# Graph layer 0: small VectorE steps on slot counts moved within the per-graph step

## The chip, the cores and the metric

One core of one Trainium2 chip runs the whole kernel. The metric is device time in microseconds (us) for one execution. TensorE (PE) does the matmuls, VectorE (DVE) the elementwise work, ScalarE (ACT) activations and copies, GpSimd (POOL) some additions, and SyncE (SP) starts the loads.

## What is computed

Four graph layers run on 128 graphs (B) of 128 nodes (N) with 64 features (F). Only layer 0 is touched. With H = 192 it is

```python
mask = (adj > 0.0).astype(x.dtype)
xj_proj = x @ W1a                                   # W1a, W1b: [64, 192]
diff = x[:, :, None, :] - x[:, None, :, :]
h = relu(xj_proj[:, :, None, :] + diff @ W1b + b1)  # one row per pair of nodes
hm = einsum('bjkh,bjk->bjh', h, mask)               # sum over the neighbours
x  = x + hm @ W2 + deg[..., None] * b2
```

where x on the right is the layer-normalised, rectified input. Since `diff @ W1b` splits into a term of the node and one of the neighbour, the kernel computes one 128x384 product a graph and then, for each node, adds up rectified sums over its neighbours.

## The kernel before, in words

**Neighbours as slots.** A node's neighbours are numbered. A chunk is eight slots (SC = 2 SU, SU = 4): a one-hot matrix per slot, made by VectorE (`dve_onehot`, L707, 128x1024), picks neighbour rows by matmul (L441, for a high and a low half-precision part) into PSUM. Four slots are a half, which fills two of the four `slot_banks`. VectorE then does `acc += min(psum, 0)` on a half: the half sum, L725. The second chunk does not start from zero: VectorE takes the difference of its one-hot from the last one (`dve_difference`, L719), so PE adds only the change. Neighbours that do not fit in a node's own chunks go to shared slots (L434 with `host`, the one-hot L713).

**The step of a graph.** Graphs come in groups of four (GS = 4), q = 0 to 3. The trace has four half sums for each of the 128 graphs, so the chunk loop (`Fori`) runs once a graph; this text calls its two half sums the loop's first and second, and the other two the last first and the last second. PE in one step: seeds from `ident` (L434), first half (eight matmuls L441), product for graph b+2 (L401), second half, `halfway`, in the loop the two halves of the difference, `between` with the transposes of the last graph's sum (L415 to L420), the shared seeds and gathers. VectorE: one-hot, one-hot of the next chunk, `gap`, difference, loop's first and second half sum, `halfway`, last first half sum, `middle`, shared one-hot, `beside`, last second half sum, `summed`, `late`, and the next graph's one-hot.

**Order and waits.** Each engine's order is as written; engines meet at semaphores. `s_free[k]` says that half k was summed, so PE can write that pair of banks again: PE's seeds of a step wait for the last second half sum of the step before, and each half of the difference waits for the half sum before it on the same banks. `s_done[k]` says that PE filled half k.

**Counting and host rows.** Beside the four steps of a group, one part a step, the kernel works out for the next group how many chunks and shared slots its nodes need: q = 0 degrees; `dve_rows` rows per candidate; PE `pe_sum_rows` (L365); `dve_full`, `dve_count_full`, `dve_own`, `dve_left`, `dve_pieces`, `dve_pads`; PE `pe_first_rows` (L371); `dve_first_rows` (start, end, shift); `dve_from_first` (L690) and `dve_host_rows` (L699), which make the 128x512 matrix `host`. PE needs `host` in `pe_host_ranks` (L386 to L393) in the fourth step. The last group has no next one, so this runs beside 31 groups. The loop over groups holds two (u = 0, 1) in each pass.

Of the kernel before, what the change touches and what calls it, by code (L numbers as in the profile page):

```python
# [12 lines left out]
def gnn_stack_kernel(nc, a, out):  # L13
# [35 lines left out]
    with ctx:  # L49
# [88 lines left out]
        degp = sb("degp", [N, GS])  # L138
        over = sb("over", [N, GS, NC])
        rounded = sb("rounded", [N, GS, NC])  # L140
# [4 lines left out]
        least = sb("least", [N, GS])  # L145
# [4 lines left out]
        end = sb("end", [N, GS])  # L150
# [141 lines left out]
        s_from = sem("rows_from_first_made")  # L292
# [322 lines left out]
        def dve_rows(dve, g):  # L615

            v = nc.vector
            dve.wait_ge(s_dc, g + 1)
            v.scalar_tensor_tensor(out=over[:, :, :], in0=pSmall[:, 0:GS].unsqueeze(2).broadcast_to([N, GS, NC]),
                                   scalar=1.0 / SS, in1=cand[:, :].unsqueeze(1).broadcast_to([N, GS, NC]),  # L620
                                   op0=ALU.mult, op1=ALU.subtract).then_inc(s_nop, 1)
            v.tensor_scalar(degp[:, :], pSmall[:, 0:GS], float(SS - 1), None, ALU.add).then_inc(s_degp, 1)
            dve.wait_ge(s_nop, 9 * g + 1)
            v.tensor_scalar(rounded[:, :, :], over[:, :, :], 1.0 / SS, WHOLE, ALU.max, ALU.add).then_inc(s_nop, 1)
            dve.wait_ge(s_nop, 9 * g + 2)
            v.tensor_scalar(rows_or[:, :, :], rounded[:, :, :], WHOLE, None, ALU.subtract).then_inc(s_rows, 1)

        def dve_full(dve, g):

            v = nc.vector  # L630
            dve.wait_ge(s_sum, g + 1)
            v.tensor_scalar(over[:, :, :], pSmall.rearrange("p (q c) -> p q c", q=GS), float(N), None, ALU.is_gt)\
             .then_inc(s_nop, 1)

        def dve_count_full(dve, g):

            v = nc.vector
            dve.wait_ge(s_nop, 9 * g + 3)
            v.tensor_reduce(nfull[:, :], over[:, :, :], AX.X, ALU.add).then_inc(s_nop, 1)

        def dve_own(dve, g):

            v = nc.vector
            dve.wait_ge(s_nop, 9 * g + 4)
            v.tensor_scalar(chunks[:, ds(g * GS, GS)], nfull[0:1, :], 1.0, None, ALU.add)

            v.tensor_scalar(own[:, :], nfull[:, :], float(SC), float(SC * MINC), ALU.mult, ALU.add).then_inc(s_nop, 1)

        def dve_left(dve, g):

            v = nc.vector
            dve.wait_ge(s_degp, g + 1)
            dve.wait_ge(s_nop, 9 * g + 5)
            v.tensor_tensor(left[:, :], degp[:, :], own[:, :], ALU.subtract).then_inc(s_nop, 1)

        def dve_pieces(dve, g):

            v = nc.vector
            dve.wait_ge(s_nop, 9 * g + 6)
            v.tensor_scalar(least[:, :], left[:, :], float(SS - 1), -1.0, ALU.max, ALU.add).then_inc(s_nop, 1)  # L660
            dve.wait_ge(s_nop, 9 * g + 7)
            v.tensor_scalar(whole[:, :], least[:, :], 1.0 / SS, WHOLE, ALU.mult, ALU.add).then_inc(s_nop, 1)
            dve.wait_ge(s_nop, 9 * g + 8)
            v.tensor_scalar(pieces[:, :], whole[:, :], WHOLE, None, ALU.subtract).then_inc(s_pieces, 1)

        def dve_pads(dve, g, p):

            v = nc.vector
            dve.wait_ge(s_pieces, g + 1)
            v.scalar_tensor_tensor(out=pad[:, :], in0=pieces[:, :], scalar=-float(SS), in1=left[:, :],  # L670
# [129 lines left out]
        with nc.Block() as block:  # L800
# [15 lines left out]
            def _(pe):  # L816
# [23 lines left out]
                def step(b, g, u, q, nxt, p, use):  # L840
# [4 lines left out]
                    def halfway():  # L845
                        if nxt is not None:
# [6 lines left out]
                            if q == 2:  # L853
                                pe_first_rows(pe, nxt)
# [863 lines left out]
```

## Time and profile before

| | us |
|---|---|
| median of 3 runs | 1464.27 |
| lowest to highest | 1462.46 to 1469.56 |
| profiled execution | 1462.28 |
| its span | 1460.6 |
| PE busy | 1320.8 (90%) |
| DVE busy | 1176.9 (81%) |
| ACT busy | 1108.5 (76%) |
| POOL busy | 498.5 (34%) |

Layer 0 fills roughly the first 1000 us. Times in a timeline count from the span's start. A row gives start, duration, engine, line, operation, what is written and read, and how many were merged; starts are the better measure of a rate, since an instruction's recorded duration reaches a little into the next. `[0.20 <-PE ...]` is idle time ahead and what ended it.

### The profile page before, as it was taken

To read this page: it belongs to the slowest core of one execution; us is meant where nothing else is said; L and a number is where in the kernel's file an instruction comes from. 1 tells how busy PE (TensorE), PEld (TensorE's weight loads), DVE (VectorE), ACT (ScalarE), POOL (GpSimd) and SP (SyncE) were. 2 spreads that over 40 slices of the span, in tenths; PEclk is the share of its full clock that TensorE was granted. 3 is DMA by queue.
4 is the path that set the end of the run, shared out by engine and by line. 5 is a ranking of instruction groups with operands and counts; after the bars stand their busy time and mean duration, and the time that the engine had idled before them with its cause. 6 is when DMAs were issued, how large, how long until landed. Compare 5 with 4: busy or idle time off the path is not lost. (4 is left out here: it accounts for less than half of the span.)

```text
span 1460.6 us, 41314 instructions
## 1 busy us (share of the span) xinstructions
PE 1320.8 (90%) x11243; PEld 1073.9 (74%) x11244; DVE 1176.9 (81%) x3034; ACT 1108.5 (76%) x2426; POOL 498.5 (34%) x611
## 2 busy tenths in 40 slices
PE   3999999999999999999999999997999997972398
PEld 1777778777787777777778777775889887910398
DVE  7899998999999998999989999984444445978755
ACT  4788888888888888888888888873555555916676
POOL 1343344443334444434344443332222111066400
PEclk9999999999999999999999999998999998986599
DMA  7000000000000000000000000000000000000022
GB/s 153 23 10 9 7 8 14 7 7 7 7 14 7 7 7 8 13 7 7 7 14 7 7 7 7 0 2 1 1 0 0 0 0 0 0 1 0 4 54 57
DMA packets 40925, 18.11 MB, mean 12 GB/s; under 512 B 19572, under 2 KB 40886, under 8 KB 40886
## 3 DMA queue, kind: packets, MB, share of 16 engines
q1 hardware_dynamic: 40354, 17.42, 4.9%
q8 instruction: 19, 0.31, 0.1%
q10 hardware_dynamic: 532, 0.21, 0.1%
q14 instruction: 20, 0.16, 0.0%
HBM read 13.44 MB, written 4.19 MB: 12 GB/s over the span
## 5 line engine op out<-in xcount | busy, mean ns | idle before, releaser
L725 DVE SCALAR_TENSOR_TENSOR acc<-slot_banks,acc 128x768 f32<-128x768 f32 x512 | 487.2, 952 | 58.2 <-PE slot_banks L441 50.8
L794 POOL TENSOR_TENSOR acc<-acc 128x384 f32<-128x384 f32 x128 | 128.2, 1001 | 551.1 <-DVE onediff L719 543.6
L441 PE MATMUL slot_banks<-ac_hi,work 128*128 128x192 f16 x1408 | 264.9, 247 | 12.1 <-DVE work L707 10.2
L441 PE MATMUL slot_banks<-ac_lo,work 128*128 128x192 f16 x1408 | 263.8, 246 | 0.0
L441 PEld LDWEIGHTS slot_banks<-ac_hi,work 128*128 (+1 forms) x1408 | 137.1, 97 | 79.1 <-issue 58.6
L441 PE MATMUL slot_banks<-ac_hi,onediff 128*128 128x192 f16 x1024 | 183.1, 246 | 2.7
L441 PE MATMUL slot_banks<-ac_lo,onediff 128*128 128x192 f16 x1024 | 182.2, 246 | 0.0
L441 PEld LDWEIGHTS slot_banks<-ac_lo,work 128*128 (+1 forms) x1408 | 138.0, 98 | 22.7 <-issue 16.9
L541 ACT ACTIVATE work<-bank 128x512 f16<-128x512 f32 x256 | 130.7, 601 | 1.2 <-PE bank L352 1.2
L780 POOL TENSOR_TENSOR ac_lo<-ac,ac_hi 128x384 f16<-128x384 f32 x128 | 118.8, 929 | 32.4 <-ACT ac_hi L581 32.4
L707 DVE TENSOR_SCALAR work<-work,slot_key 128x1024 f16 x256 | 117.6, 479 | 9.5 <-issue 1.0
L598 ACT ACTIVATE work<-slot_banks 128x576 f32<-128x576 f32 x128 | 83.4, 651 | 49.2 <-PE slot_banks L441 47.9
L589 ACT ACTIVATE acc<-ac,neg_pad 128x768 f32<-128x768 f32 x128 | 119.3, 932 | 0.0
L441 PEld LDWEIGHTS slot_banks<-ac_hi,onediff 128*128 x1024 | 104.8, 102 | 13.0 <-issue 11.3
L580 ACT ACTIVATE ac<-bank 128x384 f32<-128x384 f32 x128 | 62.2, 486 | 66.4 <-PE bank L401 66.4
L605 ACT ACTIVATE slot_banks<-ac 128x768 f32<-128x768 f32 x127 | 103.5, 815 | 11.6
L401 PE MATMUL bank<-wac,hT 65*128 65x384 f32 x256 | 109.5, 510 | 1.7 <-ACT ac_hi L581 1.1
L441 PEld LDWEIGHTS slot_banks<-ac_lo,onediff 128*128 x1024 | 100.2, 98 | 0.0
L1220 POOL TENSOR_TENSOR adjT_all<-adjT_all,ident 128x512 f32 x32 | 39.9, 1268 | 173.4 <-PE slot_banks L1174 173.4
L1141 ACT ACTIVATE onediff<-x_all,nmr,rstd 128x64 f32 (+1 forms) x256 | 90.7, 429 | 7.4 <-PE slot_banks L1312 3.2
L719 DVE TENSOR_TENSOR onediff<-work x128 | 88.5, 692 | 7.5 <-DVE work L707 0.6
L434 PE MATMUL slot_banks<-ac_hi,ident 128*128 128x384 f16 x258 | 85.1, 330 | 9.9 <-issue 8.5
(260 smaller groups left out, 3303.3 us busy)
## 6 DMA issues: line engine op xcount, KB each, us to landing
adj_in<-in_adj_dram SPq DMA_DIRECT2D x32, 256.0 KB, 2.8
out_dram<-acc SPq DMA_DIRECT2D x32, 128.0 KB, 2.0
l1w<-in_L_gnn_W_dram SPq DMA_DIRECT2D x2, 64.0 KB
l1b<-in_L_gnn_b_dram SPq DMA_DIRECT2D x2, 64.0 KB
x_all<-in_x_dram SPq DMA_DIRECT2D x4, 0.2 KB, 11.7
nm_in<-in_nodemask_dram ACTq DMA_DIRECT2D x1, 64.0 KB
w1a<-in_L_gnn_W_dram ACTq DMA_DIRECT2D x1, 48.0 KB
w1b<-in_L_gnn_W_dram ACTq DMA_DIRECT2D x1, 48.0 KB
```

The lines of the kernel that those rows point to most:

```text
L401: nc.tensor.matmul(pAC[:, 0:2 * H], hT0[:, p, q * N:(q + 1) * N], wac[:, :], start=True, stop=True)\
L434: nc.tensor.matmul(unit(pair, t, n), node, part[:, q, 0:H].unsqueeze(1).broadcast_to([N, n, H]), start=(e == 0), stop=False)
L441: last = nc.tensor.matmul(unit(pair, t, 1), hot(t), part[:, q, H:2 * H].unsqueeze(1), start=False, stop=(e == 1 and (t % SB == SB - 1 or t ...
L541: last = nc.scalar.activation(rs[:, p, :, t, :], pA3[:, :].rearrange("p (q j) -> p q j", q=GS), ACT.Copy, bias=-float(t))
L589: nc.scalar.activation(acc[:, q, :].rearrange("p (t h) -> p t h", t=SU), ac32[:, q, 0:H].unsqueeze(1).broadcast_to([N, SU, H]), ACT.Relu, ...
L605: nc.scalar.activation(unit((q + 1) % 2, 0, SU), ac32[:, q, 0:H].unsqueeze(1).broadcast_to([N, SU, H]), ACT.Copy).then_inc(s_seed, 1)
L707: nc.vector.tensor_scalar(onehot[:, ds(at, CH)], ranks.rearrange("p t j -> p (t j)"), slot_key[:, ds(key, 1)], None, ALU.is_equal).then_in ...
L719: nc.vector.tensor_tensor(onediff[:, ds(at, CH)], onehot[:, ds(at, CH)], onehot[:, ds(at_old, CH)], ALU.subtract).then_inc(s_D, 1)
L725: nc.vector.scalar_tensor_tensor(out=sums, in0=unit((q + k) % 2, 0, SU), scalar=0.0, in1=sums, op0=ALU.min, op1=ALU.add).then_inc(s_free[k ...
L780: nc.gpsimd.tensor_tensor(ac_lo[:, q, :], ac32[:, q, :], ac_hi[:, q, :], ALU.subtract)\
L794: nc.gpsimd.tensor_tensor(acc[:, q, 0:2 * H], acc[:, q, 0:2 * H], acc[:, q, 2 * H:4 * H], ALU.add)
L1141: ins = nc.scalar.activation(hn[:, u, SLOT[q] * F:(SLOT[q] + 1) * F], x[:, ds((b + q) * F, F)], ACT.Relu, bias=nmr[:, ds(b + q, 1)], scale ...
```

## The change

What `dve_rows`, `dve_full` and so on did is cut into single instructions, each put in another place. VectorE's callback `gap` (between the second one-hot and the difference) and a new one, `hole` (between the loop's two half sums), take a link each; `late` now comes behind the next graph's one-hot. The four-instruction `dve_host_rows` becomes two 128x512 ones, a comparison (`dve_inside`) and a product. One link fewer is needed for `pieces`. On PE, `pe_sum_rows` and `pe_first_rows` go from `halfway` to `between`, and `pe_h` goes behind `pe_update`.

```diff
-        def dve_pieces(dve, g):
...
-            v.tensor_scalar(least[:, :], left[:, :], float(SS - 1), -1.0, ALU.max, ALU.add).then_inc(s_nop, 1)
...
+        def dve_excess(dve, g):
...
+            return nc.vector.scalar_tensor_tensor(out=excess[:, :], in0=nfull[:, :], scalar=-float(SC) / SS,
+                                                  in1=share[:, :], op0=ALU.mult, op1=ALU.add)
+        def dve_whole():
+            return nc.vector.tensor_scalar(whole[:, :], excess[:, :], 0.0, WHOLE, ALU.max, ALU.add)
...
-        def dve_host_rows(dve, g, p):
-            dve.wait_ge(s_from, g + 1)
-            for q in range(GS):
-                rows = host[:, p, q * N:(q + 1) * N]
-                last = nc.vector.scalar_tensor_tensor(out=rows, in0=row16[:, :], scalar=end[:, q:q + 1], in1=rows,
-                                                      op0=ALU.is_lt, op1=ALU.mult)
-            last.then_inc(s_host, 1)
+        def dve_inside(dve, g):
+            dve.wait_ge(s_first, g + 1)
+            return nc.vector.tensor_tensor(inside.rearrange("p (q j) -> p q j", q=GS),
+                                           row16[:, :].unsqueeze(1).broadcast_to([N, GS, N]),
+                                           end[:, :].unsqueeze(2).broadcast_to([N, GS, N]), ALU.is_lt)
+        def dve_host_rows(p):
+            nc.vector.tensor_tensor(host[:, p, :], host[:, p, :], inside, ALU.mult).then_inc(s_host, 1)
...
                 dve_onehot(dve, rs[:, u, q, :, :], c + 1, pos)
+                gap()
...
-                gap()
                 dve.wait_ge(s_G, cnt)
                 dve_difference(dve, pos, old)
                 dve.wait_ge(s_done[0], prev)
                 dve_half(0, q)
+                dve.wait_ge(s_free[0], prev)
+                hole()
                 dve.wait_ge(s_done[1], prev)
-                dve.wait_ge(s_free[0], prev)
                 dve_half(1, q)
...
             dve_half(1, q)
             summed()
-            late()
             if not (known(b) and b == B - 1):
                 dve.wait_ge(s_rs, g1 + 1)
                 dve_onehot(dve, rs[:, p1, q1, :, :], 0, pos)
+            late()
...
                             if q == 1:
                                 pe.wait_ge(s_h, nxt + 1)
-                                pe_sum_rows(pe, nxt)
-                                pe_h(pe, nxt)
+                                pe.wait_ge(s_degp, nxt + 1)
...
+                        if nxt is not None and q == 1:
+                            pe_h(pe, nxt)
                     def between():
                         if not (known(b) and b < 1):
                             pe_transpose_sum(pe, b - 1, *group_of(b, g, u, q, 1))
...
+                            if q == 1:
+                                pe_sum_rows(pe, nxt)
+                            if q == 2:
+                                pe_first_rows(pe, nxt)
```

Where VectorE's links stand now: `halfway` rows (q = 1), pieces (2), host rows (3); `middle` own (2); `beside` full (1), left and first rows (2); `summed` count full (1), pads (2); behind the next one-hot degrees (0), negative pads (2); `gap` over (1), excess (2), from first (3); `hole` share and rounded (1), whole (2), inside (3).

VectorE in the third step of a group (q = 2), from the loop's end to the last half sum. `pieces`, `left`, `own` and `pad` are counts for the next group, `start`, `end` and `shift` come from PE's `first rows` matmul, L713 (L726 in the changed file) is the shared one-hot and L725 (L738) a half sum. Before:

```order
L771 TENSOR_TENSOR x_all<-bank,x_all 128x64
L670 SCALAR_TENSOR_TENSOR pad<-pieces,left 128x4
L725 SCALAR_TENSOR_TENSOR acc<-slot_banks,acc 128x768
L677 TENSOR_SCALAR neg_pad<-pad 128x4
L682 COPY start<-bank 128x4
L683 TENSOR_TENSOR end<-bank,pieces 128x4
L684 SCALAR_TENSOR_TENSOR shift<-bank,own 128x4
L713 TENSOR_SCALAR work<-work,slot_key 128x384
L725 SCALAR_TENSOR_TENSOR acc<-slot_banks,acc 128x768
```

and now:

```order
L785 TENSOR_TENSOR x_all<-bank,x_all 128x64
L660 TENSOR_SCALAR pieces<-whole 128x4
L738 SCALAR_TENSOR_TENSOR acc<-slot_banks,acc 128x768
L665 TENSOR_SCALAR chunks<-nfull 1x4
L666 TENSOR_SCALAR own<-nfull 128x4
L726 TENSOR_SCALAR work<-work,slot_key 128x384
L672 SCALAR_TENSOR_TENSOR left<-deg,own 128x4
L692 COPY start<-bank 128x4
L693 TENSOR_TENSOR end<-bank,pieces 128x4
L694 SCALAR_TENSOR_TENSOR shift<-bank,own 128x4
L738 SCALAR_TENSOR_TENSOR acc<-slot_banks,acc 128x768
```

The three instructions that read the matmul's result went from ahead of the shared one-hot to behind it, still ahead of the last half sum.

PE at the same place: the matmul L371 and its neighbours, the update (L426, L427) and the transposes (L415 to L420). Before:

```order
L441 MATMUL slot_banks<-ac_lo,work 128x192
L371 MATMUL bank<-pieces,before 128x4
L426 MATMUL bank<-w2a,hmTa 128x64
L427 MATMUL bank<-w2b,hmTb 128x64
```

and now:

```order
L418 MATMUL bank<-ident,acc 128x128 x2
L420 MATMUL bank<-work,hm 128x128
L371 MATMUL bank<-pieces,before 128x4
L434 MATMUL slot_banks<-ac_hi,host 128x2x192
```

The matmul moved behind the difference's sixteen matmuls and the four transposes.

VectorE in the loop of the fourth step (q = 3) before, where L278 is a layer-norm statistic and L719 the difference:

```order
L278 BN_STATS bn<-x_all 128x6
L718 ISA
L719 TENSOR_TENSOR onediff<-work 128x1024
L725 SCALAR_TENSOR_TENSOR acc<-slot_banks,acc 128x768 x2
L734 REGISTER_ALU
L734 COMPARE_AND_BRANCH
L750 TENSOR_LOAD chunks
L771 TENSOR_TENSOR x_all<-bank,x_all 128x64
L699 SCALAR_TENSOR_TENSOR host<-row,end,host 128x128 x4
```

and now:

```order
L701 TENSOR_SCALAR host<-row,start 128x128 x4
L279 BN_STATS bn<-x_all 128x6
L751 ISA
L731 ISA
L732 TENSOR_TENSOR onediff<-work 128x1024
L738 SCALAR_TENSOR_TENSOR acc<-slot_banks,acc 128x768
L708 TENSOR_TENSOR work<-row,end 128x512
L738 SCALAR_TENSOR_TENSOR acc<-slot_banks,acc 128x768
```

`from first` (L701) came in ahead of the difference and `inside` (L708) between the half sums; the four L699 behind the loop are one product now.

## Rows read from the trace of the kernel before

**Rows 1.** Timeline of PE: first seed matmul of steps (two groups).

```profile
489.07 0.33 PE L434 MATMUL slot_banks<-ac_hi,ident 128*128 128x384 f16 x1
...
519.34 0.33 PE L434 MATMUL slot_banks<-ac_hi,ident 128*128 128x384 f16 x1 [0.55 <-issue]
...
533.53 0.33 PE L434 MATMUL slot_banks<-ac_hi,ident 128*128 128x384 f16 x1
...
540.94 0.33 PE L434 MATMUL slot_banks<-ac_hi,ident 128*128 128x384 f16 x1
...
549.14 0.33 PE L434 MATMUL slot_banks<-ac_hi,ident 128*128 128x384 f16 x1
```

**Rows 2.** Timeline of PE, end of step q = 1: shared seeds start behind the transposes.

```profile
532.36 0.33 PE L434 MATMUL slot_banks<-ac_hi,host 128*128 128x384 f16 x1
```

**Rows 3.** Timeline of DVE: last half sum of q = 1, the two one-hots behind it.

```profile
532.39 0.95 DVE L725 SCALAR_TENSOR_TENSOR acc<-slot_banks,acc 128x768 f32<-128x768 f32 x1
...
534.07 1.08 DVE L707 TENSOR_SCALAR work<-work,slot_key 128x1024 f16 x2
```

**Rows 4.** Timeline of PE in the prologue: the rows matmul.

```profile
9.31 0.23 PE L365 MATMUL bank<-rows_or,ones 128*128 128x56 f16 x1
```

**Rows 5.** Timeline of DVE in the prologue: the first reader of that matmul.

```profile
9.58 0.22 DVE L632 TENSOR_SCALAR over<-bank 128x56 f32<-128x56 f32 x1 [0.32 <-PE bank L365]
```

**Rows 6.** Timeline of PE, q = 2: two halves, loop's second half, shared seeds behind the transposes.

```profile
534.69 0.25 PE L441 MATMUL slot_banks<-ac_hi,work 128*128 128x192 f16 x1 [0.34 <-DVE work L707]
...
536.03 0.25 PE L441 MATMUL slot_banks<-ac_hi,work 128*128 128x192 f16 x1
...
538.10 0.25 PE L441 MATMUL slot_banks<-ac_hi,onediff 128*128 128x192 f16 x1
...
539.86 0.33 PE L434 MATMUL slot_banks<-ac_hi,host 128*128 128x384 f16 x1
```

**Rows 7.** Timeline of DVE from the loop of q = 2 to that of q = 3.

```profile
535.95 0.95 DVE L725 SCALAR_TENSOR_TENSOR acc<-slot_banks,acc 128x768 f32<-128x768 f32 x1
537.00 0.96 DVE L725 SCALAR_TENSOR_TENSOR acc<-slot_banks,acc 128x768 f32<-128x768 f32 x1
...
539.36 0.14 DVE L684 SCALAR_TENSOR_TENSOR shift<-bank,own 128x4 f32<-128x4 f32 x1
539.43 0.30 DVE L713 TENSOR_SCALAR work<-work,slot_key 128x384 f16<-128x384 f16 x1
539.65 0.94 DVE L725 SCALAR_TENSOR_TENSOR acc<-slot_banks,acc 128x768 f32<-128x768 f32 x1
540.52 0.72 DVE L690 TENSOR_SCALAR host<-row,start 128x128 f16<-128x128 f16 x4
541.17 0.87 DVE L707 TENSOR_SCALAR work<-work,slot_key 128x1024 f16 x2
...
542.23 0.69 DVE L719 TENSOR_TENSOR onediff<-work  x1
542.84 0.95 DVE L725 SCALAR_TENSOR_TENSOR acc<-slot_banks,acc 128x768 f32<-128x768 f32 x1
543.98 0.96 DVE L725 SCALAR_TENSOR_TENSOR acc<-slot_banks,acc 128x768 f32<-128x768 f32 x1 [0.20 <-PE slot_banks L441]
```

**Rows 8.** Timeline of PE, q = 3: second half, loop's second half, host ranks.

```profile
543.12 0.25 PE L441 MATMUL slot_banks<-ac_hi,work 128*128 128x192 f16 x1
...
545.11 0.25 PE L441 MATMUL slot_banks<-ac_hi,onediff 128*128 128x192 f16 x1
...
546.93 0.38 PE L386 MATMUL bank<-row_slots,ones 128*128 128x512 f16 x1
547.14 0.38 PE L390 MATMUL bank<-host,work 128*128 128x128 f16 x4
```

**Rows 9.** Timeline of DVE, an earlier group: second of the four L699.

```profile
515.03 1.00 DVE L699 SCALAR_TENSOR_TENSOR host<-row,end,host 128x128 f16<-128x128 f16 x1
```

**Rows 10.** Timeline of POOL beside it.

```profile
514.91 0.96 POOL L780 TENSOR_TENSOR ac_lo<-ac,ac_hi 128x384 f16<-128x384 f32 x1
```

More of the change, by code:

```diff
@@ L137, in gnn_stack_kernel @@
         ranks2 = place(GS * N)
-        degp = sb("degp", [N, GS])
-        over = sb("over", [N, GS, NC])
-        rounded = sb("rounded", [N, GS, NC])
+        inside = place(GS * N)
+        over, rounded, full = (place(2 * GS * NC).bitcast(F32).rearrange("p (q c) -> p q c", q=GS) for _ in range(3))
+        deg = sb("deg", [N, GS])
+        share = sb("share", [N, GS])
+        excess = sb("excess", [N, GS])
         rows_or = sb("rows_or", [N, GS, NC], F16)
@@ L149, in gnn_stack_kernel @@
         start = sb("start", [N, GS])
-        end = sb("end", [N, GS])
+        end = sb("end", [N, GS], F16)
         shift = sb("shift", [N, GS])
@@ L612, in act_sum, with dve_degrees @@
                                  scale=unscale[0:H - N, 0:1]).then_inc(s_hmT, 1)
-        def dve_rows(dve, g):
-            v = nc.vector
+        def dve_degrees(dve, g):
             dve.wait_ge(s_dc, g + 1)
[L619 to L626, printed above, removed]
+            nc.vector.tensor_copy(deg[:, :], pSmall[:, 0:GS]).then_inc(s_degp, 1)
@@ new lines, in dve_over, with dve_round @@
+        def dve_over(dve, g):
+            dve.wait_ge(s_degp, g + 1)
+            return nc.vector.scalar_tensor_tensor(out=over[:, :, :], in0=deg[:, :].unsqueeze(2).broadcast_to([N, GS, NC]),
+                                                  scalar=1.0 / SS,
+                                                  in1=cand[:, :].unsqueeze(1).broadcast_to([N, GS, NC]),
+                                                  op0=ALU.mult, op1=ALU.subtract)
+        def dve_round(dve):
+            nc.vector.tensor_scalar(share[:, :], deg[:, :], 1.0 / SS, (1.0 - SC * MINC) / SS, ALU.mult, ALU.add)
+            return nc.vector.tensor_scalar(rounded[:, :, :], over[:, :, :], 1.0 / SS, WHOLE, ALU.max, ALU.add)
@@ L726, in dve_half, with dve_slots @@
                                            op0=ALU.min, op1=ALU.add).then_inc(s_free[k], 1)
-        def dve_slots(dve, b, g, u, q, regs, gap, halfway, middle, beside, summed, late):
+        def dve_slots(dve, b, g, u, q, regs, gap, hole, halfway, middle, beside, summed, late):
             cnt, prev, pos, old, count_reg = regs
```

131 lines of the change are left out of this document (74 added, 57 removed).

## The prediction

> **What bounds the kernel now.** The page's busy times come first (the table ahead): PE 1320.8 us of a span of 1460.6, VectorE 1176.9. Neither is full, so the question is who waits for whom in a group's four steps. The second view is PE's timeline at the first seed matmul of a step [rows 1]: it shows the period. One group runs from 519.34 to 549.14, 29.80 us; the one ahead of it, with the loop's back edge at its end, takes 519.34 - 489.07 = 30.27. Groups of either kind repeat to within 0.03 us all through layer 0, so one group times 31 is the sum. The third view sets VectorE's timeline beside PE's, to see what ends last at each meeting. I worked through the group at 519.34; the steps are called q = 0 to 3.
>
> Four delays from one engine to the other come out of the rows. From the start of a last second half sum to the seeds it frees: 533.53 - 532.39 = 1.14 us [rows 1, 3]. From a half sum's start to the difference's matmuls it frees: 545.11 - 543.98 = 1.13 [rows 7, 8]. From the start of eight matmuls to their half sum: 543.98 - 543.12 = 0.86 [rows 7, 8]. From a one-hot's start to the matmuls that need it: 534.69 - 534.07 = 0.62 [rows 3, 6]. A half sum alone keeps VectorE 540.52 - 539.65 = 0.87; where the next instruction waits for its result, 537.00 - 535.95 = 1.05 [rows 7].
>
> In q = 0 and 1 PE runs with hardly a gap. In q = 2 it waits 0.34 us for the one-hot, which stands behind the `pieces` chain [rows 6]. In q = 3 VectorE has the four L699 between the loop and the last first half sum, and PE's host ranks and shared seeds wait for that. These waits are what the change could win. So VectorE's order, not its total, matters.
>
> **q = 1: the one-hot comes earlier, the seeds later.** The link `full` reads the matmul L365. Before, that matmul was issued ahead of the loop's two halves and the result was long there. Now PE issues it after the transposes, at the place where the shared seeds began, 532.36 [rows 2]. VectorE gets to `full` before that, since before it already began the half sum behind it at 532.39, after three more instructions [rows 3]. A small matmul reaches its reader in 9.58 - 9.31 = 0.27 us in the prologue [rows 4, 5]; I take 0.25. So `full` runs at 532.61. It has the 56 elements of the prologue's and costs 0.13 (a fixed 0.07, below, and 56 elements at 1.04 ns). The half sum begins at 532.74, where it began at 532.39: 0.35 late. Queued behind the waiting `full` on VectorE are that half sum and the next one-hot; PE's seeds of q = 2 wait for them. Seeds: 532.74 + 1.14 = 533.88. They are four matmuls of 384 columns; one of 512 takes 547.14 - 546.93 = 0.21 [rows 8], which makes 0.16 to 0.17 each and 0.66 in all, so they end at 534.54. The one-hot comes at 532.74 + 0.87 + 0.12 (`count full`) = 533.73 and would let PE go on at 534.35. So the first half starts at 534.54 in place of 534.69: a gain of 0.15, from a step that lost 0.34 before.
>
> **q = 2: the half sum waits for the transposes.** PE's second half starts 536.03 - 534.69 = 1.34 later [rows 6], at 535.88. The loop's second half sum can start at 535.88 + 0.86 = 536.74 (before 537.00 [rows 7]). On VectorE's side: one-hot 533.73, then two one-hots, statistic and difference (542.84 - 541.17 = 1.67 [rows 7]) and `excess` 0.07 give the first half sum at 535.47, and `whole` after 1.05 ends at 536.59. It fits into the wait for PE. Excess and whole cost nothing here; with no cover they would cost 0.07 each. The loop's second half on PE: 536.74 + 1.13 = 537.87 (before 538.10 [rows 6], a gain of 0.23). From there to the end of the transposes PE took 539.86 - 538.10 = 1.76 [rows 6], so the end is at 539.63. Only now comes L371, and 0.25 later, at 539.88, `start`, `end` and `shift`, each 539.43 - 539.36 = 0.07 [rows 7]. Own, left and the shared one-hot before them are over by 539.1, so VectorE stands idle some 0.7 us. The last half sum begins at 540.09, where it began at 539.65 [rows 7]: 0.44 late. Behind the wait stand that half sum and the next one-hot, and all of q = 3.
>
> **q = 3: the two places hide little.** Before, the way from that half sum to the loop's first one was 542.84 - 539.65 = 3.19, all of it busy: 0.87, from first 541.17 - 540.52 = 0.65, and 1.67 [rows 7]. Now pads (0.11) and the negative pads (0.07) join it, and from first only changes its place: 3.37. The half sum starts at 543.46, 0.62 later than before. PE is ready for it: seeds 540.09 + 1.14 = 541.23, first half 541.89, plus 0.86 is 542.75. So `gap` is no wait in this step. In `hole`, `inside` starts 1.05 later, at 544.51, and its duration p stands on the path, since PE's second half is done by 541.89 + 1.34 + 0.86 = 544.09. No row shows its form (two half-precision inputs, one of them a single element repeated). The bounds are the rates of two rows: the difference, 1024 elements in 542.84 - 542.23 = 0.61, is 0.53 ns an element beyond the fixed 0.07; a half sum, 768 in 0.87, is 1.04 ns. For 512 elements p is 0.34 or 0.60. I take 0.60, the half sum's rate, as its operands too are not simply packed pairs; that is the less certain choice. The second half sum is then at 545.11, where it was at 543.98: 1.13 late. PE's difference goes on at 546.24, and from there nothing on VectorE holds it: the product for `host` (0.34, packed, at the difference's rate) is over near 546.7, ahead of the host ranks. PE's remaining work is 1.76 for the rest of the loop and the transposes, host ranks three times 547.14 - 546.93 = 0.21, so 0.64 [rows 8], and shared seeds and gathers 540.94 - 539.86 = 1.08 [rows 1, 6]: 3.48. The next group's seeds are at 549.72, before at 549.14 [rows 1]: **0.58 late**. What was won is real: the L699 chain no longer holds the last half sums. What is late next is the loop's second half sum.
>
> On this engine the Trainium skill speaks to p. By "Vector Engine (DVE) Microarchitecture Reference", section 5.1, one element read again and again as the second input of a two-source operation ran at one element a cycle; that would make p about 0.60 by the same fixed part, the value taken. No row here shows that form.
>
> **Sum.** q = 0 changes by nothing: the degree copy now behind the one-hot stands where PE has a step's slack. `pe_h` behind the update puts 0.44 us of PE work after it and takes none away. The prologue gains or loses under 0.5 us. So 31 x 0.58 = 18 us; with p = 0.34 it is 31 x 0.32 = 10 us. The profiled execution's 1462.28 becomes 1480; the median of the runs, 1464.27, lies 2 us above it, which gives **1482**.
>
> **Rivals.**
> *A, collisions with GpSimd.* The second L699 of an earlier group took 1.00 us, while GpSimd's L780 ran from 514.91 for 0.96 [rows 9, 10]: it ended just after that one. Both of its inputs are in SBUF. The links in `hole` fall in this stretch, since GpSimd's three additions begin at the difference's end, and `inside` and the halfway product have two such inputs. The second addition begins within 0.1 us of `hole`'s start, so who is first is a toss. L780 cost up to 515.87 - 515.03 = 0.84; an addition of two thirds its length about 0.4 for `inside`, and 0.3 for `pieces` and `whole` of q = 2 if they are held too. That adds 0.7 a group, 22 us: 1504.
> The skill's page "SBUF — State Buffer", section "Who interferes with whom", has it as an exclusive lock, and counts tensor_scalar in its two-port modes too, so that `whole`, `pieces` and `rounded` would be held as well. The row agrees for two inputs; nothing here shows it for the others.
> *B, p = 0.34.* 1464.3 + 10 = 1474.
> *C, the back edge is hidden.* Ahead of 549.14 PE waited on half sums in the same step; if it no longer does, its sequencer can run ahead through the branch, worth up to 30.27 - 29.80 = 0.47 in 15 groups, 7 us [rows 1]. With A and B absent 1475; with p = 0.34 as well 1467, no change.
> *D, faster: the two matmuls do not hold the half sums.* The place is `beside` in q = 1 and 2. If the matmuls L365 and L371 are there when VectorE arrives, the 0.44 of q = 2 falls away. With p = 0.34 the group is 0.12 shorter, and with the back edge hidden too the sum is 1464 - 4 - 7 = 1453. It decides from the point where the transposes end before the shared one-hot does, which needs PE 0.7 us earlier; against it is that PE's order is fixed and its second half is already bound by its own matmuls.
> *E, what the change says does not come:* that a link costs as much in `gap` as elsewhere is already in the sum for q = 3, and the one-hot directly behind the half sum wins only 0.15.
>
> **How the numbers follow.** Forecast 0.45 (1476 to 1488 by the delays' rounding and 0.1 us for small links); A in full or part 0.15; B 0.12; C with p = 0.34 about 0.14; D 0.14. A measurement of this kernel tells about 0.5%, 7 us, from no change. Faster by more than that 0.13, within 0.15, slower 0.72 (the forecast, A, B). The range runs from C, a little below the median, to just under all of A: 1463 to 1501; D and the rest of A are left out.
>
> **What would show it.** In the changed profile: VectorE idle ahead of `full` (L640) and `start` (L692), ended by PE's L365 and L371, some 0.3 and 0.7 us; no idle of PE at q = 2's first half; L708 at 0.60 in p and no wait of the half sum behind it; groups of 30.4 and 30.8 us in place of 29.80 and 30.27. I am wrong if L692 follows the shared one-hot without idle, if L708 ends before PE's second half, or if the groups are under 30 us.

## The result and the profile after

The changed kernel takes 1477.13 us (median of 6 runs, 1473.18 to 1478.59) where the kernel before took 1464.15 beside it. The ratio is 1.0077, with a 95% interval of 1.0063 to 1.0091: slower by 9 to 13 us. The forecast was 1482 in a range of 1463 to 1501. The profiled execution took 1477.16 us with a span of 1475.5.

The page of the changed kernel, section 1 and two groups of section 5 (busy us, mean ns of one, then the engine's idle time ahead of them and what ended it):

```profile
PE 1322.8 (90%) x11243; PEld 1076.7 (73%) x11244; DVE 1145.9 (78%) x3002; ACT 1112.2 (75%) x2426; POOL 515.9 (35%) x611
...
L738 DVE SCALAR_TENSOR_TENSOR acc<-slot_banks,acc 128x768 f32<-128x768 f32 x512 | 487.5, 952 | 77.5 <-PE slot_banks L441 70.7
...
L441 PE MATMUL slot_banks<-ac_hi,onediff 128*128 128x192 f16 x1024 | 185.9, 247 | 28.9 <-DVE acc L738 23.3
```

VectorE has 31 us less to do than before (1176.9), and the kernel is slower all the same. The half sums take what they took, 952 ns each. New is most of PE's idle time ahead of the difference's matmuls, which wait for a half sum: 28.9 us, where it was 2.7.

PE's timeline over a group of layer 0, with the seeds (L434 `ident`) that [rows 1] shows of before, the two small matmuls, and the two places where PE waits for VectorE:

```profile
493.51 0.33 PE L434 MATMUL slot_banks<-ac_hi,ident 128*128 128x384 f16 x1
...
524.02 0.33 PE L434 MATMUL slot_banks<-ac_hi,ident 128*128 128x384 f16 x1
...
537.11 0.19 PE L365 MATMUL bank<-rows_or,ones 128*128 128x56 f16 x1
...
538.49 0.34 PE L434 MATMUL slot_banks<-ac_hi,ident 128*128 128x384 f16 x1
...
544.22 0.17 PE L371 MATMUL bank<-pieces,before 128*128 128x4 f16 x1
...
545.67 0.34 PE L434 MATMUL slot_banks<-ac_hi,ident 128*128 128x384 f16 x1 [0.20 <-DVE acc L738]
...
550.81 0.25 PE L441 MATMUL slot_banks<-ac_hi,onediff 128*128 128x192 f16 x1 [0.69 <-DVE acc L738]
...
554.33 0.33 PE L434 MATMUL slot_banks<-ac_hi,ident 128*128 128x384 f16 x1
```

A group takes 554.33 - 524.02 = 30.31 us, before 29.80; one with the back edge 524.02 - 493.51 = 30.51, before 30.27. With 16 of the one kind and 15 of the other this is 16 x 0.51 + 15 x 0.24 = 11.8 us. In the trace the last seeds of layer 0 come 11.0 us later than before, since the prologue and the first and last groups differ a little.

VectorE's timeline of the same group, where [rows 3], [rows 7] and [rows 9] show it before: the two links that read a matmul's result, the half sums behind them, and the loop of q = 3:

```profile
537.35 0.22 DVE L640 TENSOR_SCALAR work<-bank 128x56 f32<-128x56 f32 x1 [0.40 <-PE bank L365]
537.48 0.95 DVE L738 SCALAR_TENSOR_TENSOR acc<-slot_banks,acc 128x768 f32<-128x768 f32 x1
...
544.45 0.16 DVE L692 COPY start<-bank 128x4 f32<-128x4 f32 x1 [0.61 <-PE bank L371]
544.53 0.15 DVE L693 TENSOR_TENSOR end<-bank,pieces 128x4 f16<-128x4 f32 x1
544.60 0.15 DVE L694 SCALAR_TENSOR_TENSOR shift<-bank,own 128x4 f32<-128x4 f32 x1
544.67 0.95 DVE L738 SCALAR_TENSOR_TENSOR acc<-slot_banks,acc 128x768 f32<-128x768 f32 x1
...
548.09 0.95 DVE L738 SCALAR_TENSOR_TENSOR acc<-slot_banks,acc 128x768 f32<-128x768 f32 x1
549.07 0.73 DVE L708 TENSOR_TENSOR work<-row,end 128x512 f16<-128x512 f16 x1
549.72 0.94 DVE L738 SCALAR_TENSOR_TENSOR acc<-slot_banks,acc 128x768 f32<-128x768 f32 x1
```

VectorE stands idle 0.40 us for L365 and 0.61 us for L371, both with a half sum queued behind. The comparison L708 keeps it for 549.72 - 549.07 = 0.65 us between the two half sums of the loop. All three were in the forecast.

### The profile page after: what moved, and what is told of

The parts are those of the page before. It is cut to its first block and busy times, and to the rows that moved or that the text cites. A ratio compares the mean times of both kernels' runs of the same rounds, so it can differ in the third digit from the quotient of the medians.

```text
span 1475.5 us, 41433 instructions
## 1 busy us (share of the span) xinstructions
PE 1322.8 (90%) x11243; PEld 1076.7 (73%) x11244; DVE 1145.9 (78%) x3002; ACT 1112.2 (75%) x2426; POOL 515.9 (35%) x611
## 5 line engine op out<-in xcount | busy, mean ns | idle before, releaser
L738 DVE SCALAR_TENSOR_TENSOR acc<-slot_banks,acc 128x768 f32<-128x768 f32 x512 | 487.5, 952 | 77.5 <-PE slot_banks L441 70.7
L441 PE MATMUL slot_banks<-ac_hi,onediff 128*128 128x192 f16 x1024 | 185.9, 247 | 28.9 <-DVE acc L738 23.3
L794 POOL TENSOR_TENSOR ac_lo<-ac,ac_hi 128x384 f16<-128x384 f32 x128 | 123.4, 964 | 49.5 <-ACT ac_hi L581 49.5
L441 PEld LDWEIGHTS slot_banks<-ac_hi,onediff 128*128 x1024 | 101.3, 99 | 51.0 <-issue 48.6
L434 PE MATMUL slot_banks<-ac_hi,ident 128*128 128x384 f16 x258 | 85.1, 330 | 10.3 <-DVE acc L738 6.3
```

The lines of the kernel that those rows point to most:

```text
L434: nc.tensor.matmul(unit(pair, t, n), node, part[:, q, 0:H].unsqueeze(1).broadcast_to([N, n, H]), start=(e == 0), stop=False)
L441: last = nc.tensor.matmul(unit(pair, t, 1), hot(t), part[:, q, H:2 * H].unsqueeze(1), start=False, stop=(e == 1 and (t % SB == SB - 1 or t ...
L738: nc.vector.scalar_tensor_tensor(out=sums, in0=unit((q + k) % 2, 0, SU), scalar=0.0, in1=sums, op0=ALU.min, op1=ALU.add).then_inc(s_free[k ...
L794: nc.gpsimd.tensor_tensor(ac_lo[:, q, :], ac32[:, q, :], ac_hi[:, q, :], ALU.subtract)\
```

## The experiments

Steps below are PE's, from seeds to seeds. "Group" is the sum of the four without the back edge, "last step" the q = 3 that has the back edge in it. Each ratio is to the kernel before, run beside it, whose median there was 1463.23 us for e1 to e4, 1464.92 for e5 to e8 and 1463.38 for e9 to e12.

| kernel | q=0 | q=1 | q=2 | q=3 | group | last step | median us | ratio, 95% interval |
|---|---|---|---|---|---|---|---|---|
| before | 7.31 | 6.88 | 7.41 | 8.20 | 29.80 | 8.68 | 1464.15 | |
| after | 7.38 | 7.09 | 7.18 | 8.66 | 30.31 | 8.78 | 1477.13 | 1.0077, 1.0063 to 1.0091 |
| e1 matmuls early | 7.39 | 6.90 | 7.08 | 8.62 | 29.99 | 8.78 | 1463.89 | 1.0011, 0.9997 to 1.0025 |
| e2 comparison late | 7.39 | 7.08 | 7.19 | 8.75 | 30.41 | 9.18 | 1479.89 | 1.0123, 1.0104 to 1.0142 |
| e3 both | 7.39 | 6.90 | 7.08 | 8.70 | 30.07 | 9.20 | 1468.29 | 1.0043, 1.0026 to 1.0060 |
| e4 before, one-hot alone | 7.31 | 6.88 | 7.45 | 8.21 | 29.85 | 8.68 | 1468.82 | 1.0032, 1.0021 to 1.0044 |
| e5 e1 and pieces early | 7.40 | 6.94 | 6.87 | 8.48 | 29.69 | 8.71 | 1454.29 | 0.9935, 0.9914 to 0.9956 |
| e6 readers late | 7.39 | 6.80 | 6.81 | 8.32 | 29.32 | 8.46 | 1445.25 | 0.9873, 0.9851 to 0.9896 |
| e7 e5 and from first late | 7.39 | 6.94 | 6.87 | 8.62 | 29.82 | 9.18 | 1466.87 | 1.0006, 0.9991 to 1.0021 |
| e8 after, again | | | | | | | 1473.37 | 1.0064, 1.0047 to 1.0081 |
| e9 e6 again | 7.39 | 6.80 | 6.81 | 8.33 | 29.33 | 8.47 | 1445.58 | 0.9868, 0.9836 to 0.9900 |
| e10 e6, matmuls early | 7.38 | 6.91 | 6.91 | 8.23 | 29.43 | 8.37 | 1449.14 | 0.9900, 0.9876 to 0.9924 |
| e11 e6, one-hot last | 7.39 | 6.80 | 6.93 | 8.47 | 29.59 | 8.58 | 1454.31 | 0.9933, 0.9909 to 0.9957 |
| e12 e6, comparison twice | 7.38 | 6.80 | 6.80 | 9.32 | 30.30 | 9.48 | 1481.25 | 1.0112, 1.0084 to 1.0140 |

In some kernels q = 1 and q = 2 differ by up to 0.1 us between the two kinds of groups. Of q = 3 in e12, 5 steps of 31 are longer than the table's; they are told of below.

**e1: the two matmuls ahead of the transposes.** It takes away what the two links wait for.

```diff
 def between():
+    if nxt is not None and q in (1, 2):
+        pe.wait_ge(s_x0, b - 1)
+        pe_sum_rows(pe, nxt) if q == 1 else pe_first_rows(pe, nxt)
     pe_transpose_sum(pe, b - 1, *group_of(b, g, u, q, 1))
...
-    if q == 1:
-        pe_sum_rows(pe, nxt)
-    if q == 2:
-        pe_first_rows(pe, nxt)
```

> The changed kernel with one edit: PE issues the two small matmuls (rows, first rows) right behind the loop, ahead of the four transposes instead of behind them. Theory (the last half sums of q = 1 and 2 wait for matmuls that stand behind the transposes): the idle time of VectorE ahead of its two readers (0.40 and 0.61 us) goes, q = 1 is 0.4 us shorter and q = 2 some 0.7 us, the group falls from 30.4 to 29.3 us on average, the kernel from 1477 to 1443 us, under the kernel before. Rival 1 (the moved comparison between the loop's half sums of q = 3 is the whole loss): within 5 us of 1477. Rival 2 (PE now waits for VectorE's counts at the earlier place): PE idle ahead of L365 or L371, over 1477.

It came to 1463.89, the time of the kernel before. That is 13 us under the changed kernel by the medians and 10 by the ratios, where the theory had expected 34. Both waits are gone. But VectorE now comes to two small links while GpSimd is adding. VectorE's timeline of e1 in q = 2:

```profile
535.76 0.57 DVE L656 TENSOR_SCALAR whole<-excess 128x4 f32<-128x4 f32 x1
...
537.24 0.63 DVE L660 TENSOR_SCALAR pieces<-whole 128x4 f16<-128x4 f32 x1
```

and GpSimd's beside it:

```profile
535.70 0.59 POOL L810 TENSOR_TENSOR work<-work 128x192 f32<-128x192 f32 x1
...
536.93 0.91 POOL L794 TENSOR_TENSOR ac_lo<-ac,ac_hi 128x384 f16<-128x384 f32 x1
```

Each works on four elements a partition and takes 0.20 us in the changed kernel. Here `whole` starts 0.06 us after L810 and ends with it (536.33 and 536.29); `pieces` starts inside L794 and ends with that (537.87 and 537.84). Together they lose 0.37 + 0.43 = 0.80 us; e5 tests how much of that the step pays. That is rival A's mechanism, on other instructions than the forecast named.

**e2: the comparison behind the loop.** `inside` leaves the place between the half sums.

```diff
 def hole():
-    if nxt is not None and q == 3:
-        dve_inside(dve, nxt)
 def halfway():
     if nxt is not None and q == 3:
+        dve_inside(dve, nxt).then_inc(s_in, 1)
+        dve.wait_ge(s_in, nxt)
         dve_host_rows(p)
```

> The changed kernel with one edit: the 128x512 comparison of q = 3 stands behind the loop, ahead of the product, instead of between the loop's two half sums. Theory (its 0.65 us is bare VectorE time ahead of the half sum that frees PE's last matmuls): the loop's second half sum of q = 3 starts 0.6 us earlier, PE's last wait of the step shrinks from 0.69 to about 0.1 us, a group is 0.6 us shorter, the kernel 1477 - 31 x 0.6 = 1458 us. Rival (the place between the half sums hides it, as PE is the later one there): 1477 or, as the comparison then delays the last half sums, 1480 to 1490.

1479.89, no gain at all; the theory was wrong by 22 us, and its rival (1477, or up to 1490 since the last half sums come later) holds. VectorE's timeline of e2 in q = 3 shows where the 0.65 us went:

```profile
551.69 1.94 DVE L739 SCALAR_TENSOR_TENSOR acc<-slot_banks,acc 128x768 f32<-128x768 f32 x2
...
553.70 0.93 DVE L709 TENSOR_TENSOR work<-row,end 128x512 f16<-128x512 f16 x1
554.66 1.02 DVE L715 TENSOR_TENSOR host<-host,work 128x512 f16<-128x512 f16 x1
555.61 0.94 DVE L739 SCALAR_TENSOR_TENSOR acc<-slot_banks,acc 128x768 f32<-128x768 f32 x1
```

and GpSimd's:

```profile
554.04 1.37 POOL L795 TENSOR_TENSOR ac_lo<-ac,ac_hi 128x384 f16<-128x384 f32 x1
```

The half sums of the loop stand together, and PE's difference goes on without a wait. But comparison and product now stand ahead of the last first half sum, where PE waits for VectorE too (its shared seeds come 0.48 us behind the last host rank, 0.22 in the changed kernel), and both are longer there: 0.93 in place of 0.73 and 1.02 in place of 0.48, beside a GpSimd operation that is itself stretched. And the back edge costs 9.18 - 8.75 = 0.43 us again, as in the kernel before.

**e3: both edits.** 

> Both edits at once. Theory: the two losses stand in different steps and one behind the other on VectorE, so they add: -34 and -19 us from 1477 give 1424 us, unless PE's own work ends last before that; a group then cannot be under PE's work of about 27.9 us (1400 us for the kernel), and I expect 1425 to 1435. Rival (they overlap: with VectorE early in q = 3 the comparison is hidden): no better than e1.

1468.29, where 1425 to 1435 was expected. Its q = 1 and q = 2 are those of e1, its q = 3 that of e2 to 0.05 us: the effects add, and neither is what was expected of it.

**e4: the kernel before, with the next one-hot directly behind the last half sum.** One part of the change alone:

```diff
             summed()
-            late()
             ...one-hot of the next step...
+            late()
```

> The kernel before with one part of the change alone: the next graph's one-hot directly behind the last half sum, what stood ahead of it (rows, pieces, from first) behind it. Theory (in q = 2 VectorE is the later one at the loop's first half sum, and it has the same work up to there in either order): PE's wait of 0.34 us for the one-hot goes, but the half sum comes no earlier, and the time stays at 1464 within 4 us. Rival (the one-hot sets the pace of q = 2 and 3): 0.3 to 0.4 us a group, 1452 to 1455 us.

1468.82, 0.2 to 0.4% slower, with the steps of before to 0.04 us and a layer 0 that is 1.6 us longer. The steps do not show the rest of the difference, which stays open. On the kernel before this part gives nothing, as expected.

**e5: e1, with `excess`, `whole` and `pieces` in places ahead of GpSimd's additions.** If e1's missing gain is the collisions, it comes back.

```diff
+    def opening():                    # ahead of the loop's one-hot
+        if q == 2: dve.wait_ge(s_ex, nxt); dve_whole()
+    def settle():                     # ahead of the difference
+        if q == 2: dve_pieces()
     def late():
+        if q == 1: dve_excess(dve, nxt).then_inc(s_ex, 1)
```

> e1 with the links whole and pieces of q = 2 moved out of the time in which GpSimd adds: excess behind the next graph's one-hot in q = 1, whole ahead of the second one-hot, pieces ahead of the difference. The same instructions otherwise. Theory (in e1 the two four-element tensor_scalars took 0.57 and 0.63 us in place of 0.20 because GpSimd held the memory port, which ate the gain of q = 2): they take 0.15 to 0.20 again, the last half sum of q = 2 starts some 0.6 us earlier, VectorE starts q = 3 that much earlier and, being the later one there, ends it so: 31 x 0.6 = 19 us under e1, 1445 us. Rival (the length of the two is not the cause; PE bounds q = 2): 1464, as e1.

1454.29: the first version that beats the kernel before, but with 10 us of the 19 that were expected. `whole` takes 0.17 us and `pieces` 0.15 there, q = 2 falls from 7.08 to 6.87, and the group from 29.99 to 29.69. So the collisions of e1 do stand on the path, but not with their whole 0.80 us. The last half sum of q = 2 comes 0.29 us earlier than in e1; VectorE now idles 0.18 and 0.20 us ahead of two half sums of that step, for PE's own matmuls.

**e6 and e9: the matmuls stay where the change put them, and VectorE reads them behind the last half sum.** This leaves the late matmuls and takes only the half sum out from behind the wait.

```diff
 def beside():
-    if q == 1: dve_full(dve, nxt)
     if q == 2: dve_left(dve, nxt)
-    if q == 2: dve_first_rows(dve, nxt, p)
 def summed():
-    if q == 1: dve_count_full(dve, nxt)
+    if q == 1: dve_full(dve, nxt)
     if q == 2: dve_pads(dve, nxt)
+    if q == 2: dve_first_rows(dve, nxt, p)
 def late():
+    if q == 1: dve_count_full(dve, nxt)
```

> The changed kernel with the two matmuls left behind the transposes, and their readers on VectorE moved behind the last half sum (full, count full; start, end, shift). Theory (what costs is that a half sum and the seeds it frees are queued behind the wait): as e1 in q = 1 (0.2 us), and in q = 2 PE's seeds no longer wait, but VectorE's next one-hot still comes behind start, end and shift, so q = 3 begins on VectorE 0.1 to 0.6 us earlier: 1460 to 1472 us. Rival (only the matmuls' place counts): 1477.

> The version in which TensorE's small matmuls L365 and L371 stay behind the transposes and VectorE reads their banks only behind the last half sum, once more beside its variants. It should give 1445 us again, with steps of 6.80, 6.81, 8.32 and 8.47 in groups of some 29.5 us. If its gain was a scatter of the clock, it gives 1460 or more, with the last seed of layer 0 still near 973 only in the one profile.

1445.25, and 1445.58 when run again: 1.3% under the kernel before and the fastest of the study. VectorE's timeline of e9, the part that answers to the rows of the changed kernel above:

```profile
526.27 0.20 DVE L656 TENSOR_SCALAR whole<-excess 128x4 f32<-128x4 f32 x1
...
529.12 0.94 DVE L738 SCALAR_TENSOR_TENSOR acc<-slot_banks,acc 128x768 f32<-128x768 f32 x1
529.99 0.14 DVE L679 SCALAR_TENSOR_TENSOR pad<-pieces,left 128x4 f32<-128x4 f16 x1
530.06 0.14 DVE L692 COPY start<-bank 128x4 f32<-128x4 f32 x1
```

`start` comes without idle time: by the end of the half sum its matmul has long been done. The group is 30.31 - 29.33 = 0.98 us shorter than the changed kernel's, close to the sum of its two waits, 0.40 + 0.61 = 1.01. That the two agree so well is in part luck. The edit also takes the links themselves, 0.13 us for `full` and 0.22 for the other three, from ahead of the half sums, while q = 1 and q = 2, at 6.80 and 6.81 us, are now bound by PE's own work: in e9 the seeds of q = 2 stand 523.64 - 522.31 = 1.33 us behind the half sum, where 1.00 would do. The expectation for e6, 1460 to 1472, was too careful by 15 us. It had counted a part of the gain as lost to something next in line, and nearly nothing was: `whole` takes 0.20 us and `pieces` 0.21 as a rule, and q = 3 is 0.34 shorter as well.

**e10: e6 with the matmuls early.** 

> The same version, and L365 and L371 right behind the loop's matmuls, ahead of the transposes. Theory: what costs is only that a half sum stands behind a wait of VectorE for these matmuls; where the readers come behind the last half sum, their place on TensorE decides nothing, since no half sum waits for them: 1445 us within 0.5%, steps of q=1 and q=2 at 6.80 to 6.85. Rival: the matmuls' place costs by itself (the transposes and with them the shared seeds come 0.14 later, or earlier): then 1 to 4 us off, by step q=1 and q=2 alike. Second rival: GpSimd's additions fall on whole and pieces as with early matmuls before (0.57 and 0.63 us instead of 0.21): then q=2 is 7.1 and the time 1452 to 1455.

1449.14, some 4 us over e9. That is inside the theory's 0.5%, but q = 1 and q = 2 are at 6.91 where it had 6.80 to 6.85: the first rival. The cause is on PE, in the order of its own matmuls. PE's timeline of e9 at the end of q = 1:

```profile
522.33 0.39 PE L420 MATMUL bank<-work,hm 128*128 128x128 f32 x2
522.55 0.19 PE L365 MATMUL bank<-rows_or,ones 128*128 128x56 f16 x1
522.58 0.32 PE L434 MATMUL slot_banks<-ac_hi,host 128*128 128x384 f16 x1
...
523.64 0.33 PE L434 MATMUL slot_banks<-ac_hi,ident 128*128 128x384 f16 x1
```

and of e10:

```profile
523.88 0.19 PE L365 MATMUL bank<-rows_or,ones 128*128 128x56 f16 x1
523.96 0.43 PE L415 MATMUL bank<-ident,acc 128*128 128x128 f32 x2
```

Behind the transposes L365 holds up the next matmul by 0.03 us, ahead of them by 0.08. Counted from the group's first seeds, the shared seeds and the next step's seeds come 0.09 and 0.10 us later than in e9, and PE has no idle time there. VectorE is not the cause: its last half sum of q = 1 starts at 12.85 us of the group in e10 and at 12.86 in e9.

q = 1 and q = 2 are 0.11 and 0.10 longer, q = 3 is 0.10 shorter. So the late place of the matmuls is the better one by a little, once nothing on VectorE waits for them ahead of a half sum. It explains 0.10 of the 0.66 us by which e1's group is longer than e9's; the rest goes with the readers' place, and in e10 `whole` and `pieces` take 0.20 and 0.16 us, so that the collisions of e1 are gone too.

**e11: e6 with the one-hot behind the late links again.** 

> The version with late readers, with the next one-hot behind the late links again (degrees in q=0, count full in q=1, neg pads in q=2), as it stood before the change. Theory: the one-hot waits for 0.07 to 0.15 us of small links; since TensorE waits for VectorE in these steps, the next step's half sums shift with it: 0.1 us in three steps of each of 31 groups gives 3 to 9 us more, 1448 to 1454. Rival: the one-hot has slack of over 0.2 us behind the shared seeds and TensorE's loop does not see it: 1445 within 0.3%, as the one-hot alone gave nothing on the kernel before.

1454.31, some 9 us over e9, at the top of what was expected: q = 2 and q = 3 are longer by 0.12 and 0.14. The one-hot's place, which gave nothing in e4, is worth 9 us here, with other links around it. What hides it in the kernel before was not tried.

**e12: e6 with a second comparison, which nothing reads, behind the first.** 

> The version with late readers, and in the second wait of q=3 a second comparison of 128x512 (same inputs, a tile of its own that nothing reads) behind the first: twice the disputed cost. Theory: the comparison lies in VectorE's way to the second half sum past the end of that wait, so all that is added passes on: 0.65 us in each of 31 groups, 20 us, 1465; the q=3 step goes from 8.32 to some 8.97. If the two together are held by GpSimd's additions for longer, up to 1470. Rival: the wait holds more than one comparison, and what is given back later hides the rest: under 8 us, 1445 to 1453.

1481.25, 36 us over e9 where 20 to 25 were expected. Two things are in it. VectorE's timeline of e12 (here the two comparisons are L715 and L708, the half sum L745):

```profile
522.63 0.73 DVE L715 TENSOR_TENSOR work<-row,end 128x512 f16<-128x512 f16 x1
523.28 1.07 DVE L708 TENSOR_TENSOR work<-row,end 128x512 f16<-128x512 f16 x1
524.28 0.94 DVE L745 SCALAR_TENSOR_TENSOR acc<-slot_banks,acc 128x768 f32<-128x768 f32 x1
```

and GpSimd's:

```profile
522.77 1.03 POOL L817 TENSOR_TENSOR work<-work 128x192 f32<-128x192 f32 x1
523.88 0.92 POOL L819 TENSOR_TENSOR hm<-work 128x192 f32<-128x192 f32 x1
```

The second comparison is held until GpSimd's addition ends, so it adds 524.28 - 523.28 = 1.00 us, and all of that is in the step: 9.32 - 8.33 = 0.99. The rival, that the place hides it, falls: 31 x 1.0 = 31 us. The rest is PE's clock. In 5 of the 31 steps q = 3 takes 10.74 to 10.83 us. PE's wait in one of them:

```profile
555.81 0.26 PE L442 MATMUL slot_banks<-ac_hi,onediff 128*128 128x192 f16 x1 [1.67 <-DVE acc L745]
```

and the windows of this kernel (from the span's start; ahead of the DMA share stands PE's granted clock), one of a common step and two of this:

```profile
526.00:526.80 0.80, 0.79 (x8) 0.60 (x6) 0.80 (x2) 0.00 (x0) 0.00 (x0) 1.00 0.00 0
...
555.80:556.80 1.00, 0.99 (x8) 0.94 (x9) 1.00 (x2) 0.42 (x2) 0.32 (x1) 0.61 0.00 0
556.80:557.80 1.00, 1.00 (x7) 1.00 (x6) 1.00 (x3) 0.00 (x0) 0.00 (x0) 0.50 0.00 0
```

After 1.67 us of idling PE ran at 0.50 of its clock, 1.2 in place of 2.4 GHz, for some 3 us, which cost 10.74 - 9.32 = 1.4 us; the other four steps lose 1.3 to 1.4, some 7 us in all. PE's wait is 1.65 to 1.69 us in all 31 steps, and the other 26, the one of the first window among them, were given the full clock. Why those five, the runs do not tell.

**e7: e5 with `from first` behind the loop.** It asked whether q = 3 gains when the way to the loop's first half sum is shorter.

> e5 with from first of q = 3 (four 128x128 comparisons, 0.65 us) moved from ahead of the difference to behind the loop, beside the product. Theory: the loop's half sums of q = 3 start 0.3 to 0.6 us earlier, but the product comes later, GpSimd's instructions hold the comparisons, and PE waits at the host ranks or the shared seeds again and pays the back edge there: within 6 us of e5 either way, as in e2. Rival (the gap is the only thing that counts): 31 x 0.6 = 19 us under e5.

1466.87: the gain of e5 is lost. It is 13 us over e5, twice the 6 that the theory allowed, for the reasons that it names. VectorE's timeline of e7, where `from first` takes 1.45 us for its four instructions (0.74 in the changed kernel):

```profile
544.15 1.45 DVE L705 TENSOR_SCALAR host<-row,start 128x128 f16<-128x128 f16 x4
```

and GpSimd's:

```profile
544.32 0.91 POOL L800 TENSOR_TENSOR ac_lo<-ac,ac_hi 128x384 f16<-128x384 f32 x1
```

The back edge costs 9.18 - 8.62 = 0.56 us again, too.

**e8: the changed kernel, once more.** 

> The changed kernel unchanged, beside the others on one chip. Its layer 0 took 11.0 us more than before's in the profiled runs, the rest of the span 3.9 us more, with 8 us more at the lower clock. Theory (the rest is the clock's own scatter and no effect of the change): runs from 1472 to 1479, the short ones at a mean clock of 0.969. Rival (the change itself lowers the clock later): all near 1477 with 0.966.

1473.37, a ratio of 1.0064. The profile has nearly the same layer 0 as the first (its last seeds start at 1002.14 and 1002.53 us, in the kernel before at 991.56: 10.6 and 11.0 us later), while what lies behind layer 0 took 467.4 us here, 473.0 in the first profile and 469.0 before, with the same work. That part scatters from run to run, with the clock granted, by more than any effect of the change on it that could be seen here.

## Why the prediction was right, and where it was off

Times from the group's first seeds, before [rows 1, 3, 7, 8], as forecast, and as the rows after have them:

| event | before | forecast | after |
|---|---|---|---|
| q=1: last half sum | 13.05 | 13.40 | 13.46 |
| q=2: seeds | 14.19 | 14.54 | 14.47 |
| q=2: last half sum | 20.31 | 20.75 | 20.65 |
| q=3: seeds | 21.60 | 21.89 | 21.65 |
| q=3: loop's first half sum | 23.50 | 24.12 | 24.07 |
| q=3: loop's second half sum | 24.64 | 25.77 | 25.70 |
| q=3: PE's difference | 25.77 | 26.90 | 26.79 |
| next group's seeds | 29.80 | 30.38 | 30.31 |

**The two waits: right.** Forecast idle times of about 0.3 and 0.7 us ahead of `full` and `start`; they were 0.40 and 0.61. e6 and e9 show that they and the links behind them are more than the whole loss: with the readers behind the half sums the group is 0.98 us shorter, and the loss was 0.51. This also settles rival D: the matmuls were not there when VectorE arrived.

**The comparison: right in kind, small in error.** p was taken as 0.60 with bounds of 0.34 and 0.60; it is 0.65, just outside the upper bound, so rival B falls. The page "Vector Engine (DVE) Microarchitecture Reference", section 5.1, of the Trainium skill had such an operation at one element a cycle. The trace agrees: (0.65 - 0.07) / 512 = 1.13 ns an element is near the half sum's 1.04 and twice the difference's 0.53. That time added at this place stands on the path is shown by e12. But e2 shows that moving it away gains nothing, for the step has a second meeting behind it. The forecast did not ask that.

**The delay from half sum to seeds: mis-sized.** It was read as 1.14 us [rows 1, 3]. Where PE visibly waits for the half sum it is 545.67 - 544.67 = 1.00. In the row of before, then, PE had been held by something else for the last 0.14. Together with an excess of 0.1 in the last half sum of q = 2 this put the seeds of q = 3 at 21.89 in place of 21.65; nothing came of it, since in q = 3 VectorE leads. The same error stands in PE's difference, 1.13 in place of 1.09.

**q = 0: a small miss.** It was said to change by nothing, and takes 0.07 us more in one kind of group and 0.15 in the other (7.38 and 7.46 for 7.31). No run tried why. Groups were also said to repeat to 0.03 us all through layer 0; the first six and the last two do not (28.45 to 31.75 us before), which moves the sum by under 1 us.

**The back edge: rival C came in large part.** Before, the seeds behind the branch stood 0.55 us "issue" [rows 1], and the last step was 8.68 - 8.20 = 0.48 longer. After, it is 8.78 - 8.66 = 0.12, and PE has no such idle time. What differs is PE's wait for VectorE's half sum ahead of the shared seeds, close to the branch. PE's timeline of the kernel before, the last host rank and the first shared seed:

```profile
547.36 0.39 PE L393 MATMUL bank<-ident,host 128*128 128x128 f16 x4
547.84 0.32 PE L434 MATMUL slot_banks<-ac_hi,host 128*128 128x384 f16 x1
```

and of the changed kernel:

```profile
553.04 0.39 PE L393 MATMUL bank<-ident,host 128*128 128x128 f16 x4
553.26 0.33 PE L434 MATMUL slot_banks<-ac_hi,host 128*128 128x384 f16 x1
```

The two stand 0.48 us apart before and 0.22 after. They are 0.48 apart in e2, e3, e4 and e7 as well, which pay 0.43 to 0.56 us for the branch, with idle times of 0.55 to 0.60 "issue" at the seeds; they are 0.22 apart in e1, e5, e6 and e9 to e12, which pay 0.11 to 0.23. The wait earlier in q = 3, ahead of the difference's second half, does not decide it, as e7 shows, which has such a wait and still pays 0.56. PE's timeline of e7:

```profile
453.72 0.25 PE L444 MATMUL slot_banks<-ac_hi,onediff 128*128 128x192 f16 x1 [0.39 <-DVE acc L742]
```

So the rival had the right condition: where PE no longer waits so late, most of the branch is hidden. That its sequencer then runs ahead is the rival's explanation and fits, but no view shows the sequencer. The forecast of 1482 left this out, and the rival's 1475 is nearer to the measured 1477.13. Group and branch together make the 18 us of the sum into 12: 31 x 0.51 = 15.8 less 15 x 0.27 = 4. The group with the back edge was forecast at 30.8 us and takes 30.51.

**Collisions with GpSimd: not in this kernel's way.** Rival A had `inside` held. It was the other way round: `inside` started first, at 549.07, and GpSimd's addition was stretched. GpSimd's timeline of the changed kernel:

```profile
541.26 0.59 POOL L810 TENSOR_TENSOR work<-work 128x192 f32<-128x192 f32 x1
...
549.21 1.04 POOL L810 TENSOR_TENSOR work<-work 128x192 f32<-128x192 f32 x1
```

The one at 541.26 is the same addition without a neighbour. The rival's price was real, though: it was paid by `whole` and `pieces` in e1, by the comparison and the product in e2, by `from first` in e7 and by the second comparison in e12, as soon as an edit put them beside a GpSimd operation. The page "SBUF — State Buffer", section "Who interferes with whom", of the Trainium skill has tensor_scalar held as well; e1 and e7 show that (0.57, 0.63 and 1.45 us, above), where no row shown of before did.

**What the change won** was said to be real, and was: e6 differs from the changed kernel only by where five small links stand, and is 1.3% under the kernel before. Of the some 19 us between the two the earlier one-hot is worth 9 (e11); how the rest divides between the shorter host rows and the other moves was not tried. The change lost because links that read late matmuls stood ahead of half sums.

## What to carry to other kernels

An instruction that waits for another engine must stand behind the one that the rest waits for: four small links moved behind a half sum, and a fifth behind the next one-hot, turned 0.8% slower into 1.3% faster, with all instructions unchanged. When one wait is taken out of a loop, follow the step to its next meeting of the two engines before counting a gain (e2, e7), and look at what follows it: in both, PE waited again just ahead of the loop's branch and paid for the branch as well. A link moved by some tenths of a microsecond can fall into or out of a GpSimd operation that holds it to its end, so look at both timelines together.

## What the runs showed of the hardware

- A VectorE tensor_scalar of four elements a partition, 0.15 to 0.20 us in other places, took 0.57 and 0.63 us beside GpSimd operations in e1; four of 128 took 1.45 in place of 0.74 (e7); a 128x512 comparison took 1.07 in place of 0.73 (e12). It goes both ways: GpSimd's 128x192 addition took 1.04 in place of 0.59 (changed kernel). The half sums, one input of which is in PSUM, took 0.94 to 0.96 us in every kernel, beside GpSimd or not.
- The loop's branch cost PE 0.43 to 0.56 us in the five kernels in which it waited for VectorE ahead of the shared seeds, 1.8 us before the seeds behind the branch, and 0.11 to 0.23 in those in which it did not. A wait of 0.39 us earlier in the step (e7) did not change that.
- A small matmul of 56 columns held up PE's next matmul by 0.03 us behind the transposes (e9) and by 0.08 ahead of them (e10).
- A wait of 1.65 to 1.69 us on PE was followed by half the granted clock in 5 of 31 steps (e12), at 1.3 to 1.4 us each, and by the full clock in the other 26.
